# An attention and expert block, one core: the MLP's output in two halves, one sum behind three maxima, and transposes ahead of two projections

## What is computed

```
x = x + layernorm(attn(layernorm(x)))
x = x + layernorm(ffn(layernorm(x)))
attn(h): x = ln1(h); self attention, causal, 16 heads of 8; h = h + a @ wo
         x = lnx(h); cross attention over 256 encoder tokens with a key bias; h = h + a @ wxo
         x = ln2(h); h = h + gelu(x @ fc) @ mlp_proj        (512 inner features)
ffn(z):  one shared expert and 8 routed ones, the best 2 by a softmax; each silu(z @ a) * (z @ b) @ w2
```

## Time and profile before

| | us |
|---|---|
| median of 3 runs | 1694.81 |
| lowest, highest | 1693.2, 1696.81 |
| the profiled execution | 1692.39 |
| its span in the trace | 1690.6 |
| PE busy (share of the span) | 1426.2 (84%) |
| DVE busy | 1116.9 (66%) |
| ACT busy | 981.9 (58%) |
| POOL busy | 319.2 (19%) |

### The profile page before, as it was taken

The page is one execution under the profiler, slowest core; times in us unless marked ns, Lnnn a source line. Parts: engine busy times, 40 slices in busy tenths (PEclk is TensorE's granted clock), DMA queues, the critical chain, the costliest instruction groups (busy, mean ns, idle before and its releaser), DMA issues. The chain is left out here.

```text
span 1690.6 us, 39028 instructions
## 1 busy us (share of the span) xinstructions
PE 1426.2 (84%) x15448; PEld 881.3 (52%) x15448; DVE 1116.9 (66%) x3235; ACT 981.9 (58%) x1585; POOL 319.2 (19%) x428
## 2 busy tenths in 40 slices
PE   1667798889898889889888888989889898989867
PEld 1445564655556465555546465555646555554433
DVE  5657676766767676776767677676767667646334
ACT  3154674765757575675747476574747656572632
POOL 3421121211212121111212111131212102020120
PEclk7588999999999999999999999999999999997988
DMA  5414213122130402212040312203040211010000
GB/s 91 82 23 52 56 19 57 17 43 37 24 55 9 70 10 42 31 34 46 14 65 9 52 22 43 37 20 59 9 66 14 38 30 34 3 30 4 13 7 7
DMA packets 79214, 58.05 MB, mean 34 GB/s; under 512 B 11004, under 2 KB 78902, under 8 KB 79030
## 3 DMA queue, kind: packets, MB, share of 16 engines
q1 hardware_dynamic: 76420, 53.96, 18.8%
q10 hardware_dynamic: 2610, 1.58, 0.7%
HBM read 11.57 MB, written 4.19 MB: 9 GB/s over the span
## 5 line engine op out<-in xcount | busy, mean ns | idle before, releaser
L969 DVE TENSOR_REDUCE chunkmax<-ps 128x3 f32<-128x384 f32 (+1 forms) x1024 | 507.5, 554 | 128.2 <-PE ps L1273 122.8
L690 ACT ACTIVATE probs<-ps 128x768 f32<-128x768 f32 (+1 forms) x512 | 404.4, 810 | 141.8 <-PE ps L1268 137.9
L1336 PE MATMUL ps<-zT,w 128*128 128x512 f32 x576 | 277.7, 600 | 2.5 <-ACT silu_a L707 2.5
L707 ACT ACTIVATE silu_a<-ps,b 128x512 f32<-128x512 f32 x144 | 98.8, 686 | 200.3 <-PE ps L1336 200.1
L1253 PE MATMUL ps<-k_op,q_op 48*128 48x256 bf16 x512 | 147.7, 290 | 61.4 <-DVE chunkmax L969 44.0
L1235 PE MATMUL ps<-q_op,k_op 51*128 51x256 bf16 x512 | 142.5, 278 | 43.4 <-ACT probs L690 16.3
L1090 DVE SCALAR_TENSOR_TENSOR h_open<-ps,b,silu_a 128x512 f32<-128x512 f32 x128 | 95.9, 749 | 120.7 <-PE ps L1336 116.3
L1336 PEld LDWEIGHTS ps<-zT,w 128*128 128x128 f32 x576 | 105.0, 191 | 111.0 <-issue 97.3
L1362 PE MATMUL ps<-hT,w 128*128 128x512 f32 x288 | 149.1, 598 | 12.3 <-DVE hT L1096 12.3
L1253 PE MATMUL ps<-xk_op,xq_op 51*128 51x256 bf16 x512 | 144.2, 283 | 4.5 <-DVE chunkmax L969 4.1
L1265 PE MATMUL ps<-mask_q_lo,ident_lo 64*128 64x256 bf16 x512 | 146.3, 288 | 0.0
(11 more groups left out here) (235 smaller groups left out, 3426.5 us busy)
## 6 DMA issues: line engine op xcount, KB each, us to landing
q_op<-q_parts SPq DMA_DIRECT2D x192, 64.0 KB
xq_op<-xq_parts SPq DMA_DIRECT2D x192, 64.0 KB
k_op<-k_parts SPq DMA_DIRECT2D x168, 64.0 KB
x_tm<-in_L_attn_hidden_states SPq DMA_DIRECT2D x16, 256.0 KB, 5.9
x_keep<-in_L_attn_hidden_states SPq DMA_DIRECT2D x16, 256.0 KB, 6.1
out<-o_tm SPq DMA_DIRECT2D x16, 256.0 KB, 2.3
k_op<-k_parts ACTq DMA_DIRECT2D x24, 64.0 KB
w<-in_L_ffn_rw SPq DMA_DIRECT2D x1, 1024.0 KB
```

The costliest lines, as they stand in the source:

```text
L690: act.activation(probs[:, four % 2, 2 * pair:2 * pair + 2, 0:T + a.seen], ps[:, 2 * (g % 2):2 * (g % 2) + 2, 0:T + a.seen], ACT.Exp).then_ ...
L969: dve.tensor_reduce(chunkmax[:, b, at, :], ps[:, MAX_BANK[n], 0:3 * a.seen].rearrange("p (c n) -> p c n", c=3), AX.X, ALU.max).then_inc(a. ...
L1336: pe.matmul(ps[:, bank, :], w, src[:], start=True, stop=True).then_inc(sig.sem, 1)
```

## The change

It has three parts, all of order.

1. **The MLP's output in two halves.** Tiles 0 and 1 stay in bank 5, tiles 2 and 3 go to bank 1, and each half has its own signal. On DVE, `mlp_residual` takes the place of `add_residual` and `norm_stats` for h3 and n_post: per half a sum of 128x256 and two statistics, then the rest of n_post. It stands behind `stats_x`; `stats_y` comes behind it. PE waits for both sums (`free_mlp`) before the cross phase, which writes bank 1 in its first step.
2. **The sum h1 behind three maxima.** DVE's order is now three maxima, h1's sum, five maxima, the cross norm's statistics, eight maxima. It was the sum, six maxima, the statistics, ten maxima.
3. **PE's order behind the cross phase.** The transposes of x1_tm come ahead of `up_a` and `up_b` of the shared expert, and `up_a` of expert 1 ahead of `context_T`.

```diff
-        mlp_ps, h3_sb = signal("mlp_ps", 1), signal("h3_sb", 1)
+        mlp_ps, h3_sb = signal("mlp_ps", 2), signal("h3_sb", 2)
...
+            def mlp_residual(banks, j):
+
+                dve.wait_ge(*h2b_ready.done(j))
+                for half in range(2):
+                    own = slice(2 * half, 2 * half + 2)
+                    dve.wait_ge(*mlp_ps.part(j, half + 1))
+                    dve.tensor_tensor(h3[:, own, :].rearrange("p t f -> p (t f)"), ps[:, banks[half], 2 * half * D:(2 * half + 2) * D],
+                                      h2b[:, own, :].rearrange("p t f -> p (t f)"), ALU.add).then_inc(h3_sb.sem, 1)
+                    dve.wait_ge(*h3_sb.part(j, half + 1))
+                    for t in (2 * half, 2 * half + 1):
+                        dve.bn_stats(sty[:, t, :], h3[:, t, :]).then_inc(n_post.stats.sem, 1)
+                dve.wait_ge(*n_post.stats.done(j))
...
                 if exists(i + 2):
                     stats_x(i + 2)
+                if exists(k):
+                    mlp_residual((5, 1), k)
+                if exists(i + 2):
                     stats_y(i + 2)
-                if exists(k):
-                    add_residual(5, h3, h2b, mlp_ps.done(k), h2b_ready.done(k), h3_sb)
+
+                if exists(i + 1) and i > 0:
+                    maxima(sa, i + 1, 0, 3)
                 if exists(i):
                     add_residual(4, h1, yb_tm, sa.o_ps.done(i), yb_ready.done(i), sa.h)
-
-                if exists(k):
-                    norm_stats(n_post, h3, h3_sb.done(k), sty, mvy, tiny_post, k)
                 if exists(i + 1) and i > 0:
-                    maxima(sa, i + 1, 0, 6)
+                    maxima(sa, i + 1, 3, 8)
                 if exists(i):
                     norm_stats(ca, h1, sa.h.done(i), st2, mv2, tiny2, i)
                 if exists(i + 1) and i > 0:
-                    maxima(sa, i + 1, 6, 16)
+                    maxima(sa, i + 1, 8, 16)
...
-                            last = pe.matmul(ps[:, 5, t * D:(t + 1) * D], geluT[:, c, t * 128:(t + 1) * 128], wmlp[:, c, :],
+                            last = pe.matmul(ps[:, (5, 1)[t // 2], t * D:(t + 1) * D], geluT[:, c, t * 128:(t + 1) * 128], wmlp[:, c, :],
                                              start=(c == 0), stop=(c == NC - 1))
-                    last.then_inc(mlp_ps.sem, 1)
+                        if t % 2:
+                            last.then_inc(mlp_ps.sem, 1)
...
                     pe.wait_ge(*n_end.out.done(i - 3))
+                free_mlp()
                 if i > 0:
...
                     by_feature(3, wxq[:], xT, ca.q_ps)
-                if exists(k):
-                    up_a(k, 0)
-                    pe.wait_ge(*route.part(k, 1))
-                    up_b(k, 0)
                 if exists(i + 2):
                     pe.wait_ge(*sa.x_ready.done(i + 2))
                     if exists(i):
                         pe.wait_ge(*ca.xT_sb.done(i))
                     transposes(ps[:, 2, :], x1_tm, sa.xT_ps)
+                if exists(k):
+                    up_a(k, 0)
+                    pe.wait_ge(*route.part(k, 1))
+                    up_b(k, 0)
+                if exists(i + 2):
...
+                if exists(k):
+                    up_a(k, 1)
                 if exists(i - 1):
...
                 if exists(k):
-                    up_a(k, 1)
                     pe.wait_ge(*gate_split.done(k))
```

More of the change, by code:

```diff
@@ L1019, in norm_stats @@
                 dve.tensor_scalar(t[:, 2, :], mv[:, :, 0], -1.0, None, ALU.mult).then_inc(n.var_eps.sem, 1)
+            def mlp_residual(banks, j):
[9 more added lines that the diff above has]
+                dve.wait_ge(*n_post.stats.done(j))
+                dve.memset(wait_slot[:], 0.0)
+                for t in range(NB):
+                    dve.bn_aggr(mvy[:, t, :], sty[:, t, :]).then_inc(n_post.aggr.sem, 1)
+                dve.wait_ge(*n_post.aggr.done(j))
+                dve.wait_ge(*n_post.out.before(j))
+                dve.tensor_scalar(tiny_post[:, 0, :], mvy[:, :, 1], EPS, None, ALU.add).then_inc(n_post.var_eps.sem, 1)
+                dve.tensor_scalar(tiny_post[:, 2, :], mvy[:, :, 0], -1.0, None, ALU.mult).then_inc(n_post.var_eps.sem, 1)
             def over_e(x):
@@ L1474, in body @@
                     by_feature(3, wxq[:], xT, ca.q_ps)
+                if exists(i + 2):
+                    pe.wait_ge(*sa.x_ready.done(i + 2))
+                    if exists(i):
+                        pe.wait_ge(*ca.xT_sb.done(i))
+                    transposes(ps[:, 2, :], x1_tm, sa.xT_ps)
                 if exists(k):
@@ L1479, in body @@
                 if exists(i + 2):
-                    pe.wait_ge(*sa.x_ready.done(i + 2))
-                    if exists(i):
-                        pe.wait_ge(*ca.xT_sb.done(i))
-                    transposes(ps[:, 2, :], x1_tm, sa.xT_ps)
                     if exists(i):
```

## The result

The changed kernel takes 1685.81 us (median of seven runs, 1679.84 to 1688.31), the kernel before beside it 1693.23 (seven runs, 1691.85 to 1696.81). The medians are 7.4 us apart. The ratio, worked out from the single runs and not from the medians, is 0.9945 with a 95% interval of 0.9927 to 0.9963, that is 9.3 us; either way the kernel is faster, and its time lies inside the range of 1672 to 1695. The forecast of -12.3 us is a ratio of 0.993, at the interval's edge. So two things have to be explained: why most of the gain is there, and where the rest of it went (4.9 us by the medians, 3.0 by the ratio).

The account below looks back on a forecast made before the run. No engine alone was taken as the bound; cross-phase handoffs and PE among the experts decide. Eleven bodies at -1.5 + 0.55 and body 2 at -1.8 sum to -12.3 us, giving 1682.5, range 1672 to 1695.

Parts of the forecast that it names:

- The transposes and up projections: Post stage behind the cross phase: xT copy and h_open 0.97 earlier, PE's reordering gains 1.5 us per body.
- the bounds: Limits of the post stage gain: 0.97 if ACT's and DVE's run leads, 1.83 if DVE did not hold up_b.
- the rival with 0.97 in the end: Post stage gives only ACT's 0.97 per body, as DVE's casts could hold more than h_open: 1689 us, 18%.
- The MLP in halves: DVE ahead of the cross phase: first half's sum and statistics in idle time, first maximum 0.98 us earlier.
- the feared 0.6: Body 16, no output projection covering PE's wait for the second half's sum: up to 0.6 us lost, once.
- the price per instruction: DVE's fixed latency per instruction: by that rule alone, halves would lose a sixth of a microsecond per body.
- xn late through POOL: Cross phase: cross norm's statistics 0.56 later, so POOL's xn and PE's step 19 too; 0.55 us lost per body.
- xn does not decide: Rival at step 19: DVE's own maximum holds xn's statistics, giving a 0.3 gain per body: 1673 us, 12%.
- Body 14: Bodies 14 and 15 have no stats_y, so the xn term was taken as nothing there.
- Body 2's further -0.3: Body 2, where POOL has no o_tm yet: a gain of 0.3 us in place of the xn loss.
- The clock falls at the longer wait of step 19: Rival: PE's clock falls there for the rest of a cross phase, several microseconds per body: beyond 1720 us, 1%.
- Bodies 14 to 17: Post stage without x1_tm to transpose; up_a of expert 1 waits for silu in either order: nothing.

Follow-up runs that it names:

- the run with yb_tm behind it: The changed kernel with POOL's yb_tm sum moved behind o_tm and xn: 1665.72 us, ratio 0.9836 against the kernel before.
- step 3 filled: The kernel before with ten matmuls of masks put into PE's wait at step 3 of the cross phase: 1694.53 us, ratio 0.9996.

## Why the prediction was right, and what it missed

**The transposes and up projections: right.** Offsets from the router logits: the copy xT 0.97 earlier, h_open of expert 1 0.97 (both as forecast), and up_b of expert 2 does wait for it (the four matmuls at 852.44 take 2.26 in place of 1.88), so that the stage's gain is 1.46 (1.5; the third part alone gives 1.46 too). The choice between the bounds, made by the row of h_open, was the right one: the rival with 0.97 in the end would have shown periods near 96.4.

**The MLP in halves: right for the place, with one wrong detail.** The first maximum came 0.95 earlier (forecast 0.98), with the first half under the MLP. In body 16 the feared 0.6 was not lost: PE's first cross matmul waits there for ACT, 0.48 before and 0.56 now, and the halves' sum is done by then. The Trainium skill's Perfetto Trace Analysis (Optimizing Scalar/DVE Operations) says that breaking up instructions may let work be done sooner where a vector engine isn't saturated but causes bubbles elsewhere; this case agrees, with 0.34 to 0.57 per body gained, and it stands against the price per instruction that was weighed in the prediction. What the 0.16 of extra busy time cost by itself no run shows.

**xn late through POOL: right.** Behind the MLP's start, the cross norm's statistics came 0.58 later, xn's sum 0.58 later and step 19 0.57 later (forecast 0.56, 0.56 and 0.55). The rival "xn does not decide" is out by the run with yb_tm behind it. What the term hid is that it was a sum of two parts of opposite sign: halves -0.34, h1's sum behind three maxima +0.91. I worked both out in one chain of DVE's times and gave them one price, so the text doesn't say that the change would be better without its second part, by 0.91 per body and, with the falls, by some 14 us (0.9862 against 0.9945 of 1693). The rows said so: two maxima more ahead of the cross norm's statistics, each 0.465.

**Body 14: missed, small.** The forecast gave bodies 14 and 15 no loss, since they have no `stats_y`. But body 14 still has the second part: its last full interval is 1.0 shorter where the post stage gives 1.46. Two more maxima stand ahead of the cross norm's statistics, and DVE waits 0.34 for PE behind h1's sum.

**The sum over the twelve intervals.** By the forecast 12 x (-1.5) + 11 x 0.55 = -11.95; measured without falls -10.8. The difference is 0.06 in each of eleven bodies and 0.5 in body 14. Body 2's further -0.3 lies ahead of the first logits, where the scatter of the start hides it.

**The step that failed: "The clock falls at the longer wait of step 19" (1%).** It took 4.2 us between the two profiled executions, and the gain of the changed kernel with its wait filled, measured without a trace's luck, is 13.1 us (0.9923 of 1695.2) where the forecast was 12.3 and the change itself gave 7.4 in its series (9.3 by its ratio). I excluded it with one row: PE idle for 1.57 at step 3, granted clock 1.00 from 812 to 838, "no longer than one already borne". Three things were wrong with it.

First, one body is not twelve. In six others of the kernel before the clock did fall behind that same wait. This is one, PE at step 3 and behind it, then the windows of the stretch:

```profile
427.39 0.28 PE L1253 MATMUL ps<-k_op,q_op 48*128 48x256 bf16 x1 [1.57 <-DVE chunkmax L969]
...
431.35 0.39 PE L1253 MATMUL ps<-k_op,q_op 48*128 48x256 bf16 x1
```

```profile
428.00:429.00 1.00, 1.00 (x22) 0.68 (x19) 1.00 (x3) 0.89 (x2) 0.20 (x1) 1.00 0.00 0
...
429.50:430.00 0.50, 0.50 (x10) 0.20 (x9) 0.50 (x4) 0.22 (x2) 0.00 (x0) 0.50 0.00 0
...
431.00:432.50 1.50, 1.50 (x24) 0.91 (x18) 1.34 (x5) 1.31 (x4) 1.22 (x3) 0.50 0.00 0
```

The clock goes to 0.50 at 429.4 or so, 2 us behind the wait, and the matmuls take 0.39. It had cost so little (0.15 to 0.33, periods of 97.0 between those of 96.76) that it passed for scatter of the periods.

Second, the wait was priced at 1.6 us in that rival and at 1.9 in the list of what to look for; it came out at 1.95. The second number is the right one (0.92 more than before, since PE arrives earlier and the maximum comes later), and by it the comparison with 1.57 doesn't hold.

Third, the size. I took a fall to last for the rest of the cross phase and put the time beyond 1720; it lasted some 3 us and cost 0.5 to 1.5, in half of the bodies. As an all or nothing it deserved a small chance; as 4 us on the forecast it should have been in the sum. The Trainium skill's TensorE: Matmul & The Clock Gate (What's actually happening) has idle time returning the engine to 1.2 GHz; I held the 1.57 against it. The trace agrees with the page after all, with 0.50 granted from 442 to 444 behind the 1.95, and in the kernel before with 0.50 from 431 to 432.5.

**Bodies 14 to 17.** The forecast had nothing for them. What the last interval gained beyond the halves' 0.7 is a fall behind PE's wait of 1.96 in body 17, which both profiles of the old order have (59.49, and 59.51 with step 3 filled). The third part splits that wait. With the first two parts and not the third it stays whole, and no fall came; no run was made that fills it. For the forecast this 1.6 is luck: no term had it, and it took back part of what the falls behind step 19 cost.

**What stays open:** which bodies of an execution have a fall. It differs between equal bodies of one execution, and may well differ between executions: the runs of the changed kernel spread over 8.5 us (1679.84 to 1688.31), the two quickest at a mean clock of 0.955 and the profiled one at 0.951. But only one of them has a trace.

## What to carry to other kernels

When the most loaded engine waits for a value, read the whole in-order queue of the engine that delivers it, however idle that engine is over the span: here 1.27 us of unhurried work ahead of xn on POOL, busy for 19%, cost 1.14 per body, and moving one statement was worth some 19 us. Price each part of an edit apart, even when one chain of times gives their sum; the second part of this change was a loss that the first one covered. And when PE will wait longer somewhere, look at its granted clock behind the nearest such wait in every body, not in one: a wait may cost once by its length and again by the slower matmuls behind it.

## What was not expected of the hardware

A wait of 1.95 us of PE was followed in six of twelve bodies by about 3 us at a granted clock of 0.50, at 0.5 to 1.5 us each. Twelve matmuls of no use, 1.47 us in that wait, took all of the falls away, and the ratio went from 0.9945 to 0.9923 (the intervals overlap, so the proof is the periods and the clock of the runs). Behind step 3's wait of 1.57 the level fell 0.4 to 2 us later (in the body shown when PE had been at work again since 427.39: 0.88 from 429.0, 0.50 from 429.5), and stayed down for about 3 us as well, but cost only 0.25. Why the same three microseconds cost several times as much behind step 19 wasn't tried by itself, but the rows show what takes them up. In a body without a fall PE waits for DVE twice more between step 3 and step 19; the first of these waits is this one:

```profile
819.48 0.28 PE L1253 MATMUL ps<-k_op,q_op 48*128 48x256 bf16 x1 [0.55 <-DVE chunkmax L969]
```

The second is the 1.03 at 826.34. In the body with the fall at 429.4 the 0.55 is gone and step 19 has this:

```profile
438.75 0.28 PE L1253 MATMUL ps<-k_op,q_op 48*128 48x256 bf16 x1 [0.81 <-DVE chunkmax L969]
```

So step 19 comes 11.36 behind step 3 in place of 11.11: the slower matmuls grew into waits that PE had anyway. Behind step 19 of the changed kernel DVE leaves PE only a wait of 0.22, and the next one, 1.17 for ACT, is as long with a fall in the body shown (453.10) as without one.
